# The skip term of a Mamba-2 mixer: from TensorE's products with a diagonal to a ScalarE copy and GpSimd arithmetic

## The chip, the cores and the metric

The kernel runs on one NeuronCore of a Trainium2 chip, as one program. The metric is the device time in microseconds (us), the median of three runs. The core has five instruction streams: TensorE (PE, matrix products into PSUM), VectorE (DVE), ScalarE (ACT), GpSimd (POOL) and SyncE (SP, which issues most DMAs). Each executes its own instructions in the order in which they are written; between engines, an instruction waits on semaphores that others raise.

## The reference, cut to what matters

One transformer block on `x` of shape (2, 4096, 256): an adaptive layer norm, a Mamba-2 mixer with a gated linear unit (GLU) and a layer norm, a gated residual, then a mixture-of-experts layer with 16 experts, 4 chosen per token. The change touches only the mixer's skip term. There `xs` (512 channels, 8 heads of 64) comes out of a causal convolution and a SiLU, and a state-space scan runs over each head:

```
h = h * dA[:, :, None, None] + dti[:, :, None, None] * xi[..., None] * Bi[:, None, None, :]
y = jnp.einsum('bhpn,bn->bhp', h, Ci)
...
y = jnp.transpose(ys, (1, 0, 2, 3)) + D_skip[None, None, :, None] * xh      # the skip term
y = y * jax.nn.silu(z)
y = y * jax.lax.rsqrt(jnp.mean(y * y, axis=-1, keepdims=True) + EPS) * rms_w
return y @ W_out
```

`D_skip` is one number per head, so the skip term scales each head's 64 channels of `x` by one number.

## The kernel before, in words

The program has four stages. The first prepares weights and the normed, transposed input (0 to about 150 us). The second is the mixer, to about 1250 us; the change lies there. The third runs the experts on rows gathered by DMA, and the fourth adds everything up.

The mixer works on groups of 256 tokens, 16 groups for each of the two sequences (b = 0, 1), each group cut into two chunks of 128 tokens (c = 0, 1). Its order of work is written out by hand. The function `halves` calls `half(first, second, tail, ...)` once for each step of a pipeline, and every engine has its own `half`, which says in which order that engine does its parts. In one half three groups are in flight: `first` is projected and convolved, `second` runs the scan, and `tail` does the output projection, the GLU and the second norm. The sequences take turns, so there are 32 halves with a `second`. Other arguments add routing work: `routed` groups get their expert logits, `chosen` picks the experts for two groups at once (every other half, from group 3 on), and `sent` scatters a group's rows to the experts' tables with eight indirect DMAs that GpSimd issues (`scatter`, from group 4 on).

I call the 13 halves with both `sent` and `chosen` first-kind halves, the 13 with `sent` and no `chosen` second-kind ones, and the six halves of groups 1 to 3 early ones.

Within the scan, chunk-wise: TensorE turns `cv` (x after the convolution, channels on partitions) into x by token in PSUM, in the bank `Q(b, c)`. VectorE makes `xdt` (x times dt) and `xend` from that bank. ScalarE puts exponentials into `dec`, VectorE multiplies them by C·B (`times_decay`), and TensorE's `within` writes the part of y inside the chunk back into `Q(b, c)`. The part of y that comes from the state (`from_state`, bank `Q(b, 2)`) is scaled by VectorE into `yy` (`scale_from_state`). `add_within` adds the bank to `yy`. Then GpSimd multiplies by silu(z) (`gate_y`), ScalarE squares and sums, VectorE scales the sum (`mean_square`), GpSimd takes the root (`root_y`), ScalarE scales y (`norm_y`), and TensorE turns it (`transpose_y`).

Before the change, `within` starts with four fp32 products per chunk: `cv` times `skip_w`, a diagonal of D made in the first stage. They add D·x into the same bank as the rest, so y needs no other instruction for it.

VectorE's order in a half, around the change: `times_decay` 0, `scale_from_state` 0, `new_state` 0 (waits for GpSimd's `decay_state`), `times_decay` 1, `add_within` 0, `scale_from_state` 1, `apply2` of the tail (two instructions from PSUM, L1452, then two from SBUF, L1459), `mean_square` 0, `add_within` 1, `conv` of the first group's pair 0, `mean_square` 1. TensorE's `project_xbc` 1 waits for `apply2`.

## Time and profile before

| | us |
|---|---|
| median of 3 runs | 1898.64 (1896.55 to 1900.88) |
| the profiled execution | 1901.73 |
| its span, first to last instruction | 1899.9 |
| TensorE busy, whole span | 1612.4 (85%) |
| VectorE busy | 1337.1 (70%) |
| ScalarE busy | 1113.9 (59%) |
| GpSimd busy | 990.0 (52%) |

A profile records one execution. An instruction's row has a start and a duration; a row of several instructions that follow each other on an engine shows their count and their joint duration. The duration of an instruction that waited inside the engine for a resource contains this wait. Idle time before an instruction is given in brackets with what ended it. In the page's second part the span is cut into 40 slices of 47.5 us, each digit a tenth.

### The profile page before, as it was taken

The numbers are of one execution on the slowest core, as the hardware profiler recorded it, in microseconds if no ns is written. First come the engines' busy times: TensorE is split into PE (matmuls) and PEld (weight loads), VectorE is DVE, ScalarE is ACT, GpSimd is POOL, SyncE is SP. The second block draws the span as 40 slices with busy tenths as digits, with TensorE's granted clock in tenths as the row PEclk, the third lists the DMA queues.
The fourth block names the chain that finished last, engine by engine and source line by source line (L and its number), as shares of the span: only waits on it lengthen the run. The fifth ranks groups of instructions, "written<-read, shape, count | busy, mean of one in ns | idle before, by whom it ended". The sixth has DMA issues, their size and how long they took to land. (4 is left out here: it accounts for less than half of the span.)

```text
span 1899.9 us, 36188 instructions
## 1 busy us (share of the span) xinstructions
PE 1612.4 (85%) x10868; PEld 1389.8 (73%) x10868; DVE 1337.1 (70%) x3293; ACT 1113.9 (59%) x2270; POOL 990.0 (52%) x938
## 2 busy tenths in 40 slices
PE   6752899999999999999999999742999999995877
PEld 5751677777787777777777777631999999993554
DVE  6641688888888888888888888534555555553777
ACT  2322576767767676767767676533777777771211
POOL 1200333465656566565656565655666666673332
PEclk8556999999999999999999999855999999996999
DMA  7413010121212212121212121157766666647785
GB/s 255 155 47 118 15 43 32 48 72 61 78 61 74 68 60 76 66 71 64 77 59 78 64 64 67 62 189 207 231 202 213 213 200 212 212 137 300 293 303 210
DMA packets 147626, 240.27 MB, mean 126 GB/s; under 512 B 25500, under 2 KB 94364, under 8 KB 147136
## 3 DMA queue, kind: packets, MB, share of 16 engines
q1 hardware_dynamic: 122096, 168.45, 27.5%
q0 software_dynamic: 25344, 69.50, 10.1%
q8 instruction: 97, 1.59, 0.4%
q14 instruction: 89, 0.73, 0.1%
HBM read 130.51 MB, written 109.48 MB: 126 GB/s over the span
## 5 line engine op out<-in xcount | busy, mean ns | idle before, releaser
L2004 POOL DMA_INDIRECT ys_dram<-byo,bids x272 | 260.6, 958 | 141.2 <-ACT byo L1933 98.2
L1358 DVE SCALAR_TENSOR_TENSOR cv<-xc,convw,cv 128x256 f32<-128x256 f32 x576 | 300.4, 589 | 41.3 <-ACT cv L1218 41.3
L912 POOL DMA_INDIRECT xs_dram<-rows,dest x256 | 264.5, 1033 | 77.7 <-issue 66.9
L1966 DVE TENSOR_TENSOR bff<-bgs,bank 128x256 f32<-128x256 f32 x136 | 57.3, 421 | 148.2 <-ACT bgs L1916 148.2
L133 PE MATMUL bank<-wh,bhh 128*128 x544 | 154.3, 284 | 0.0
L135 PE MATMUL bank<-wh,bhl 128*128 x544 | 153.9, 283 | 0.0
L134 PE MATMUL bank<-wl,bhh 128*128 x544 | 153.7, 283 | 0.0
L133 PE MATMUL bank<-hTh,win_hi 128*128 128x256 f32 x384 | 116.2, 303 | 42.6 <-POOL hTl L1543 39.2
L1257 ACT ACTIVATE xdt<-yy 128x512 f32<-128x512 f32 x64 | 40.3, 629 | 158.7 <-POOL yy L1556 158.7
L1556 POOL TENSOR_TENSOR yy<-yy,zs 128x512 f32<-128x512 f32 x64 | 87.7, 1371 | 70.7 <-DVE yy L1399 70.2
L1933 ACT ACTIVATE byo<-bank,bws 128x256 f32<-128x256 f32 x272 | 114.3, 472 | 17.2 <-PE bank L135 1.4
L1086 PE MATMUL bank<-xdt,dec 128*128 128x64 f32 x1024 | 121.6, 272 | 1.7 <-DVE dec L1384 1.7
L1957 DVE TENSOR_TENSOR bhl<-bank,bhh 128x512 fp32r<-128x512 f32 x136 | 94.1, 692 | 38.5 <-ACT bhh L1909 23.6
L1086 PEld LDWEIGHTS bank<-xdt,dec 128*128 128x128 f32 x1024 | 119.5, 192 | 2.1 <-DVE dec L1384 2.1
L133 PEld LDWEIGHTS bank<-hTh,win_hi 128*128 128x128 f32 x384 | 73.3, 191 | 57.7 <-issue 50.9
L1842 PE MATMUL bank<-ident,bx 128*128 128x128 f32 x544 | 82.6, 275 | 32.2 <-DMA bx<-xs_dram 32.2
L134 PE MATMUL bank<-hTl,win_hi 128*128 128x256 f32 x384 | 109.1, 284 | 0.0
L135 PE MATMUL bank<-hTh,win_lo 128*128 128x256 f32 x384 | 109.0, 284 | 0.0
L1218 ACT ACTIVATE cv<-bank,convb,convw 128x256 f32<-128x256 f32 x192 | 97.7, 562 | 10.5 <-PE bank L135 10.5
L133 PEld LDWEIGHTS bank<-wh,bhh 128*128 128x128 f32 x544 | 103.1, 189 | 0.4 <-issue 0.4
L134 PEld LDWEIGHTS bank<-wl,bhh 128*128 128x128 f32 x544 | 103.1, 190 | 0.0
L135 PEld LDWEIGHTS bank<-wh,bhl 128*128 128x128 f32 x544 | 103.0, 189 | 0.0
(262 smaller groups left out, 5343.8 us busy)
## 6 DMA issues: line engine op xcount, KB each, us to landing
bx<-xs_dram SPq DMA_DIRECT2D x272, 129.0 KB
cy<-ys_dram SPq DMA_DIRECT2D x32, 1024.0 KB, 8.3
px<-in_x SPq DMA_DIRECT2D x16, 512.0 KB
h_t<-phT SPq DMA_DIRECT2D x16, 512.0 KB, 4.0
hT<-h_t SPq DMA_DIRECT2D x32, 256.0 KB
xr<-in_x SPq DMA_DIRECT2D x32, 256.0 KB
x_dram<-xr SPq DMA_DIRECT2D x32, 256.0 KB, 2.0
h_dram<-h SPq DMA_DIRECT2D x32, 256.0 KB, 2.5
```

The lines of the kernel that those rows point to most:

```text
L133: pe.matmul(out, a_hi, b_hi, start=start, stop=False, skip_group_check=True)
L134: pe.matmul(out, a_hi, b_lo, start=False, stop=False, skip_group_check=True)
L135: return pe.matmul(out, a_lo, b_hi, start=False, stop=stop, skip_group_check=True)
L912: pool.indirect_dma_start(out=xs_dram[:, :], out_offset=bass.IndirectOffsetOnAxis(ap=dest[p][:, CH * b + c, k:k + 1], axis=0), in_=rows[b] ...
L1086: last = pe.matmul(Q(b, c)[:, h * HD:(h + 1) * HD], dec[b][:, c, h, :], xdt[b][:, c, h * HD:(h + 1) * HD], start=False, stop=True, skip_gr ...
L1218: last = act.activation(cv[b][:, n, :], Q(b, pair)[:, m * GROUP:(m + 1) * GROUP], ACT.Identity, bias=convb[:, n:n + 1], scale=convw[:, n, ...
L1358: dve.scalar_tensor_tensor(cv[b][:, m, :], xc[b][:, m, tap:tap + GROUP], convw[:, m, tap:tap + 1], cv[b][:, m, :], ALU.mult, ALU.add).then ...
L1556: pool.tensor_tensor(y, y, zs[b][:, c, :], ALU.mult).then_inc(y4_done[b], 1)
L1842: last = pe.transpose(XT[u % 2][:, (k * 2 + n) * P:(k * 2 + n + 1) * P], x[u % XBUF][:, n, k * P:(k + 1) * P], ident[:, :])
L1933: last = act.activation(yo[u % YBUF][:, n, :], DN[u % 2][:, n * D:(n + 1) * D], ACT.Copy, scale=ws[u % XBUF][:, n:n + 1])
L1957: dve.tensor_tensor(hl[u % 2][:, :, :, :].rearrange("p k n t -> p (k n t)"), XT[u % 2][:, :], hh[u % 2][:, :, :, :].rearrange("p k n t -> ...
L2004: pool.indirect_dma_start(out=ys_dram[:, :], out_offset=bass.IndirectOffsetOnAxis(ap=ids[u % XBUF][:, n:n + 1], axis=0), in_=yo[u % YBUF][ ...
```

## The change

ScalarE copies x by token from `Q(b, c)` to a new SBUF tile `skip` (4 KiB a partition, shared by both sequences). GpSimd multiplies it in place by D per head (`times_skip`) and adds it to the state's part of y in `yy` (`add_skip`). TensorE's `within` no longer has the four products; its first product opens the bank. VectorE's `add_within` waits for `add_skip` instead of for its own `scale_from_state`. GpSimd's scatter of six rows is cut into four before the scan's parts and two after them. In the first stage four VectorE instructions that made the diagonal are gone, and a constant of 8 columns is loaded in place of one of 4.

```diff
 def prepare_tokens
-                        for m in range(KI):
-                            dve.tensor_scalar(skip_w[:, m, :], ident[:, :], dcol[:, m:m + 1], None, ALU.mult)
...
 within (PE)
                     pe.wait_ge(xend_done[b], CH * i + c + 1)
-                    for m in range(KI):
-                        pe.matmul(Q(b, c)[:, m * P:(m + 1) * P], cv[b][:, m, c * P:(c + 1) * P], skip_w[:, m, :],
-                                  start=(m == 0), stop=False, skip_group_check=True)
+                    pe.wait_ge(xk_done[b], CH * i + c + 1)
                     pe.wait_ge(w_done[b], CH * i + c + 1)
                     for h in range(H):
                         last = pe.matmul(Q(b, c)[:, h * HD:(h + 1) * HD], dec[b][:, c, h, :],
-                                         xdt[b][:, c, h * HD:(h + 1) * HD], start=False, stop=True,
+                                         xdt[b][:, c, h * HD:(h + 1) * HD], start=(h == 0), stop=True,
...
 ACT
+                def copy_x(b, i, c):
+                    act.wait_ge(xend_done[b], CH * i + c + 1)
+                    act.wait_ge(skip_done[1 - b], 2 * CH * (i + b))
+                    act.activation(skip[:, c, :], Q(b, c)[:, :], ACT.Copy).then_inc(xk_done[b], 1)
...
                     if second:
                         decays(*second, 1)
-                    if second:
+                        copy_x(*second, 0)
+                        copy_x(*second, 1)
                         copy_b(*second)
...
 add_within (DVE)
-                    dve.wait_ge(y1s_done[b], CH * i + c + 1)
+                    dve.wait_ge(skip_done[b], 2 * CH * i + CH + c + 1)
                     dve.wait_ge(yin_ps[b], CH * i + c + 1)
...
 POOL
+                def times_skip(b, i, c):
+                    pool.wait_ge(xk_done[b], CH * i + c + 1)
+                    x = skip[:, c, :].rearrange("p (h e) -> p h e", h=H)
+                    pool.tensor_tensor(x, x, d_head[:, :].unsqueeze(2).to_broadcast([P, H, HD]),
+                                       ALU.mult).then_inc(skip_done[b], 1)
+
+                def add_skip(b, i, c):
+                    pool.wait_ge(skip_done[b], 2 * CH * i + c + 1)
+                    pool.wait_ge(y1s_done[b], CH * i + c + 1)
+                    pool.tensor_tensor(yy[b][:, c, :], yy[b][:, c, :], skip[:, c, :], ALU.add).then_inc(skip_done[b], 1)
...
                     if sent:
-                        scatter(pool, *sent, slice(2, 8))
+                        scatter(pool, *sent, slice(2, 6))
                     if early:
                         scatter(pool, *early, slice(0, EARLY))
                     if second:
+                        times_skip(*second, 0)
+                        times_skip(*second, 1)
                         decay_state(*second, 0)
                     if tail:
                         root_norm2(*tail)
                     if second:
+                        add_skip(*second, 0)
                         gate_y(*second, 0)
+                        add_skip(*second, 1)
                         root_y(*second, 0)
                         gate_y(*second, 1)
                         root_y(*second, 1)
+                    if sent:
+                        scatter(pool, *sent, slice(6, 8))
```

GpSimd's order in one half with `sent`, from the second scatter call, which follows `shift_x`, to the next `decay_state`, before. `state` is `decay_state`, `rs` the roots of the norms, `yy<-yy,zs` is `gate_y`, `rr` is `root_y`, DMA is a scatter:

```order
L912 DMA xs_dram<-rows,dest 135168x258 x6
L1550 TENSOR_TENSOR state<-state,par 128x512
L900 TENSOR_TENSOR rs<-rs,minus_half 128x2
L1556 TENSOR_TENSOR yy<-yy,zs 128x512
L900 TENSOR_TENSOR rr<-rr,minus_half 128x1
L1556 TENSOR_TENSOR yy<-yy,zs 128x512
L900 TENSOR_TENSOR rr<-rr,minus_half 128x1
L1550 TENSOR_TENSOR state<-state,par 128x512
```

The same stretch in the changed kernel. `skip<-skip,d_head` is `times_skip`, `yy<-yy,skip` is `add_skip`:

```order
L912 DMA xs_dram<-rows,dest 135168x258 x4
L1560 TENSOR_TENSOR skip<-skip,d_head 128x512 x2
L1554 TENSOR_TENSOR state<-state,par 128x512
L900 TENSOR_TENSOR rs<-rs,minus_half 128x2
L1566 TENSOR_TENSOR yy<-yy,skip 128x512
L1571 TENSOR_TENSOR yy<-yy,zs 128x512
L1566 TENSOR_TENSOR yy<-yy,skip 128x512
L900 TENSOR_TENSOR rr<-rr,minus_half 128x1
L1571 TENSOR_TENSOR yy<-yy,zs 128x512
L900 TENSOR_TENSOR rr<-rr,minus_half 128x1
L912 DMA xs_dram<-rows,dest 135168x258 x2
L1554 TENSOR_TENSOR state<-state,par 128x512
```

Two scatters have moved from before the scan's parts to behind `root_y` 1, ahead of the tail's `decay_state`. Two products stand before `decay_state` 0, one sum between the root and `gate_y` 0, and one sum between `gate_y` 0 and `root_y` 0.

TensorE's order from the tail's `transpose_y2` (`y`) through `from_state` (`state,cv`), `state_add` (`xend,bg`) and `within` (`xdt,dec`) to the first product of `project_xbc` 1 (L133), before:

```order
L1143 MATMUL bank<-ident,y 128x128 x4
L1097 MATMUL bank<-state,cv 128x512
L1104 MATMUL bank<-xend,bg 128x512
L1082 MATMUL bank<-skip_w,cv 128x128 x4
L1086 MATMUL bank<-xdt,dec 128x64 x8
L1097 MATMUL bank<-state,cv 128x512
L1082 MATMUL bank<-skip_w,cv 128x128 x4
L1086 MATMUL bank<-xdt,dec 128x64 x8
L133 MATMUL bank<-hTh,win_hi 128x256
```

And in the changed kernel:

```order
L1141 MATMUL bank<-ident,y 128x128 x4
L1095 MATMUL bank<-state,cv 128x512
L1102 MATMUL bank<-xend,bg 128x512
L1084 MATMUL bank<-xdt,dec 128x64 x8
L1095 MATMUL bank<-state,cv 128x512
L1084 MATMUL bank<-xdt,dec 128x64 x8
L133 MATMUL bank<-hTh,win_hi 128x256
```

The four products per chunk are gone; nothing else has moved on TensorE. On ScalarE the two copies stand between the exponentials of chunk 1 and `copy_b`, and VectorE's order in the mixer is the same as before.

## Rows read from the trace of the kernel before

**Rows 1.** The page's busy shares and the granted clock in 40 slices.
```profile
PE 1612.4 (85%) x10868; PEld 1389.8 (73%) x10868; DVE 1337.1 (70%) x3293; ACT 1113.9 (59%) x2270; POOL 990.0 (52%) x938
...
PEclk8556999999999999999999999855999999996999
```

**Rows 2.** Busy us of each engine in 650 to 850 us (columns: us; engines; clock).
```profile
650.00:850.00 200.00, 186.51 (x1255) 154.40 (x1256) 171.71 (x417) 141.16 (x282) 121.56 (x117) 1.00 0.21 69
```

**Rows 3.** Groups by line, 400 to 1100 us: count, busy us, mean ns, idle.
```profile
L1082 PE MATMUL bank<-skip_w,cv 128*128 128x128 f32 x336 | 44.3, 275 | 0.0
```

**Rows 4.** ScalarE in order of time: start, duration, instruction, idle before it.
```profile
715.09 0.60 ACT L1242 ACTIVATE bg<-bank 128x512 f32<-128x512 f32 x1 [1.04 <-PE bank L1049]
```

**Rows 5.** VectorE in order of time, a first-kind half, then a second-kind one.
```profile
720.67 0.69 DVE L1405 TENSOR_TENSOR state<-state,bank 128x512 f32<-128x512 f32 x1 [0.40 <-POOL state L1550]
721.27 1.22 DVE L1384 TENSOR_TENSOR dec<-dec,bg 128x1024 f32<-128x1024 f32 x1
722.41 0.68 DVE L1399 TENSOR_TENSOR yy<-yy,bank 128x512 f32<-128x512 f32 x1
...
724.51 0.88 DVE L1459 SCALAR_TENSOR_TENSOR xr<-sg,rs,xr 128x256 f32<-128x256 f32 x2
...
725.56 0.69 DVE L1399 TENSOR_TENSOR yy<-yy,bank 128x512 f32<-128x512 f32 x1
726.16 3.51 DVE L1358 SCALAR_TENSOR_TENSOR cv<-xc,convw,cv 128x256 f32<-128x256 f32 x6
...
753.64 0.69 DVE L1405 TENSOR_TENSOR state<-state,bank 128x512 f32<-128x512 f32 x1 [1.41 <-POOL state L1550]
...
755.38 0.68 DVE L1399 TENSOR_TENSOR yy<-yy,bank 128x512 f32<-128x512 f32 x1
...
758.34 0.68 DVE L1399 TENSOR_TENSOR yy<-yy,bank 128x512 f32<-128x512 f32 x1
```

**Rows 6.** GpSimd in order of time, the same two halves.
```profile
719.07 1.49 POOL L1550 TENSOR_TENSOR state<-state,par 128x512 f32<-128x512 f32 x1
720.53 0.72 POOL L900 TENSOR_TENSOR rs<-rs,minus_half 128x2 f32<-128x2 f32 x1
723.17 1.27 POOL L1556 TENSOR_TENSOR yy<-yy,zs 128x512 f32<-128x512 f32 x1 [1.92 <-DVE yy L1399]
...
726.32 1.48 POOL L1556 TENSOR_TENSOR yy<-yy,zs 128x512 f32<-128x512 f32 x1 [0.24 <-DVE yy L1399]
...
750.06 0.96 POOL L912 DMA_INDIRECT xs_dram<-rows,dest  x1 [0.30 <-issue]
...
752.49 1.05 POOL L1550 TENSOR_TENSOR state<-state,par 128x512 f32<-128x512 f32 x1
```

**Rows 7.** TensorE in order of time, the same two halves.
```profile
723.55 1.90 PE L1086 MATMUL bank<-xdt,dec 128*128 128x64 f32 x16
...
758.41 0.39 PE L133 MATMUL bank<-hTh,win_hi 128*128 128x256 f32 x1 [0.28 <-DVE xr L1459]
```

**Rows 8.** VectorE: a conv pass alone, a `dec` product that waited, all of L1358 (min/median/max).
```profile
700.93 2.47 DVE L1358 SCALAR_TENSOR_TENSOR cv<-xc,convw,cv 128x256 f32<-128x256 f32 x6
...
652.08 2.60 DVE L1384 TENSOR_TENSOR dec<-dec,bg 128x1024 f32<-128x1024 f32 x1
...
L1358 DVE SCALAR_TENSOR_TENSOR cv<-xc,convw,cv x576: 468/477/1722, 182.7 to 1198.3; 128x256 f32<-128x256 f32 x192
```

**Rows 9.** GpSimd's state decay behind VectorE's `dec` product, an early half.
```profile
293.81 1.91 POOL L1550 TENSOR_TENSOR state<-state,par 128x512 f32<-128x512 f32 x1 [5.63 <-PE bank L1097]
```

**Rows 10.** VectorE in the same early half.
```profile
293.60 1.22 DVE L1384 TENSOR_TENSOR dec<-dec,bg 128x1024 f32<-128x1024 f32 x1
...
295.83 0.69 DVE L1405 TENSOR_TENSOR state<-state,bank 128x512 f32<-128x512 f32 x1 [0.40 <-POOL state L1550]
...
297.57 0.68 DVE L1399 TENSOR_TENSOR yy<-yy,bank 128x512 f32<-128x512 f32 x1
...
300.86 0.69 DVE L1399 TENSOR_TENSOR yy<-yy,bank 128x512 f32<-128x512 f32 x1 [0.24 <-PE bank L1086]
```

14 lines of the change are left out of this document (8 added, 6 removed).

## The prediction, made before the changed kernel ran

> **What bounds the kernel now.** I began with the busy shares and the clock. TensorE is the busiest engine, 85% of the span, and in the mixer every slice but the first ones shows its full granted clock [rows 1]. A stretch in the middle of the mixer gives 186.5 us of TensorE in 200, VectorE 171.7, ScalarE 141.2, GpSimd 121.6 [rows 2]. So TensorE looks like the bound, and GpSimd looks 39% free. Both shares mislead, and the next views show why.
>
> The timeline tells which wait ends last. TensorE starts `project_xbc` 1 at 758.41 when VectorE's `apply2` releases it [rows 7]. In the first-kind half it ends `within` 1 at 725.45 (723.55 + 1.90) [rows 7], as `apply2` ends at 725.39 (724.51 + 0.88) [rows 5]. VectorE meanwhile goes from instruction to instruction with little idle time, and waits 0.40 and 1.41 us before `new_state` 0 for GpSimd's `decay_state` [rows 5]. So the path through this part of a half is VectorE's queue with GpSimd's in it: `decay_state` 0, `new_state` 0, `times_decay` 1, `add_within` 0, `gate_y` 0, the squares, `mean_square` 0, `add_within` 1, then the convolution and everything of the next half behind it. I measure by three marks, each a VectorE start: s = `new_state` 0, a = `add_within` 0, e = `add_within` 1. In the first-kind half a - s is 1.74 and e - a is 3.15; in the second-kind half 1.74 and 2.96 [rows 5]; in the early half 1.74 and 3.29 [rows 10].
>
> There is a second thing that no busy share shows. A VectorE instruction with both inputs in SBUF and a GpSimd tensor instruction do not run together. A convolution pass of six instructions takes 2.47 us alone [rows 8], and 3.51 us [rows 5] where `gate_y` 1 (726.32, 1.48 us) lies beside it [rows 6]. The difference is 1.04 us, and the median of these instructions is 0.477 us with a longest one of 1.722 [rows 8]. It goes the other way too: `decay_state` takes 1.05 us where VectorE waits idle [rows 5, 6], but 1.91 us behind `times_decay` 0, which starts 0.21 us before it and lasts 1.22 [rows 9, 10]; it ends 0.90 us after it. Where VectorE reads PSUM nothing waits: `gate_y` 0 takes 1.27 us [rows 6]. Durations of busy engines contain such waits, so the 39% are not free.
>
> **What is removed.** Eight products a half leave TensorE. The group has 336 records in 21 halves and 44.3 us of busy time [rows 3], 2.11 us a half, 67.5 us over 32 halves. Inside the half they lie ahead of the two `within`, and TensorE then waits for `times_decay` or for `apply2`. Neither s nor a depends on them. Mark e does in some halves: if the product before `within` 1 goes, this release comes about 0.9 us earlier, but I find below that GpSimd then releases later. So I count 0 for the removal. The four VectorE instructions of the first stage and the constant's size are nothing that a row could show.
>
> **ScalarE's two copies.** They cost like `copy_b`, 0.60 us each with some overlap, 1.1 us together, and stand where ScalarE waits 1.04 us for TensorE before `copy_b` at 715.09 [rows 4]. They push `copy_b` by about 0.1 us. Its reader `times_decay` 0 comes over 2 us later. I count 0. Without that gap it would be 1.1 us of ScalarE, which has idle time later in the half.
>
> **GpSimd, up to s.** The two `times_skip` are products of the form of `decay_state` (128x512, one factor broadcast): 1.05 alone, up to 1.49 where it meets VectorE [rows 6]. They take the time of two scatters, 2.43 us (750.06 to 752.49) [rows 6], so GpSimd's queue itself is even. But scatters ran beside VectorE without delaying it, and the products don't. In the second-kind half `times_skip` 0 would run from about 749.8 to 750.8, when VectorE reaches `times_decay` 0 (about 750.4). Two orders are possible. If VectorE gets its turn after the first product, `decay_state` ends about 0.23 us later than now. If GpSimd keeps on through the second product and `decay_state`, VectorE's product and the scaling behind it come first before s, 0.8 us late. A row shows the second kind of order: at 652.08 `times_decay` took 2.60 us, 1.38 too many, behind GpSimd [rows 8]. In the first-kind half the products end at about 718.6, as `times_decay` 0 begins, and the same two orders give 0.08 and 0.55. I take 0.3 and 0.4 for the two kinds, the nearer to the smaller, since the waiting case occurs once in this trace. In early halves GpSimd is idle before `decay_state`, 5.63 us [rows 9], and I take 0.
>
> The Trainium skill ("SBUF — State Buffer", section "Who interferes with whom") says that the pair of SBUF ports shared by VectorE and GpSimd goes to whichever instruction issues first, for its whole length. The row at 652.08 is no clean case of that. By the page alone this term would be 0.08 and 0.23, and the sum 5 us smaller.
>
> **From s to a.** Now `root_norm2` (0.72 us, 720.53) ends at 721.25 [rows 6], where VectorE starts `times_decay` 1 (721.27) [rows 5], and `add_within` 0 follows at 722.41. After the change `add_skip` 0 issues at that same moment, and `add_within` 0 needs both. Both read two SBUF tiles, so they run one after the other. `add_skip` has the form of `gate_y`: 1.27 us [rows 6]. With GpSimd first, VectorE's product is delayed by that less its own start, 1.05. With VectorE first, `add_skip` ends 1.12 us after it (the 0.90 measured above plus the 0.22 by which it is longer), and with 0.1 us for the semaphore and the 0.08 by which VectorE's own instructions overlap, `add_within` 0 is 1.31 us late. I take 1.2, between ends that are close, for all 32 halves.
>
> **From a to e.** `gate_y` 0 starts 0.76 us after a (723.17 - 722.41) and ends at a + 2.03 [rows 5, 6]. `add_skip` 1 follows at once, and `apply2`'s two SBUF instructions start at a + 2.10 (724.51) [rows 5]. They wait until `add_skip` 1 ends at a + 3.3, which costs what the convolution loses to `gate_y` now, 1.04. Where nothing else delayed e it stood at a + 2.96, so e becomes a + 4.0: later by 1.04 in second-kind halves, 0.85 in first-kind and 0.71 in early ones. If VectorE went first, `add_skip` 1 would end after `apply2`, at about a + 4.2, and add 0.2. TensorE's release of `project_xbc` 1 moves with `apply2`, so none of this is taken up there.
>
> **Behind e.** `root_y` 0 now stands behind `add_skip` 1, but ends in time for `gate_y` 1, which waits for e anyway. The two moved scatters (2.4 us) come behind `root_y` 1, and then the tail's `decay_state`. In the second-kind half this ends near VectorE's next SBUF convolution, and could cost up to 0.5 there. VectorE has idle time behind this convolution, so I take 0 and keep 0.5 for the upper end.
>
> **The sum.** Early halves: 1.2 + 0.71 = 1.9 us. First-kind: 0.3 + 1.2 + 0.85 = 2.35. Second-kind: 0.4 + 1.2 + 1.04 = 2.65. Then 6 x 1.9 + 13 x 2.35 + 13 x 2.65 = 11.4 + 30.6 + 34.5 = 76.4 us. Against the profiled execution, 1901.73 (span 1899.9), that is 1978. The median of the runs is 3.1 us below this execution; carried over, the forecast is 1975 us. With all lower ends the halves are 1.76, 1.98 and 2.32, together 66.5 us. With all upper ends they are 1.31 + 0.91 = 2.22, 0.55 + 1.31 + 1.05 = 2.91 and 0.8 + 1.31 + 1.24 + 0.5 = 3.85, together 101 us. The likeliest case's own range is 1965 to 2000.
>
> **The rivals.**
> *No exclusion for the new instructions.* If the sums ran beside VectorE, the chain on GpSimd would still be longer. a would move to the end of `add_skip` 0, s - 0.1 + 0.72 + 1.27 + 0.1 = s + 2.0, 0.25 late, and e to a + 3.4, 0.1 to 0.45 late. With 0.5 us a half over 32 halves that is 16 us: 1915. Against it stand the convolution and `decay_state` rows; for it only that no row shows `add` against `times_decay`. 8%.
> *The collisions partly hide.* One of the two sums finds a gap, because the halves settle into other phases. Then a half loses 1.0 to 1.3 us, 37 us, 1936. 10%.
> *TensorE is the bound.* The share of 93% [rows 2] speaks for it, and the wait of `add_within` 1 for `within` in early halves, where e - a is 3.29 [rows 10]. If all 2.11 us came off each half, 1831 us. It decides if GpSimd's four new instructions end before VectorE needs them, that is if `add_skip` 0 ends by s + 1.7; it issues at s + 0.6 and lasts 1.27. TensorE's waits for `apply2` speak against it. 4%.
> *The clock falls.* TensorE has longer pauses afterwards: one of about 2 us between `within` 1 and `project_xbc` 1, another before `within` 1. Its granted clock is at 2.4 GHz through the mixer now, at half of that in the slices around 1235 to 1330, behind the mixer's end where TensorE is little used [rows 1]. If one half in four ran at 1.2 GHz, its 28.6 us of TensorE (186.5 / 200 of the 32.97 between the two a of rows 5, less 2.11) would take 57, some 22 us over its new length of 35.4, and 8 such halves would bring 176 us on top of the forecast: 2151. No row in the steady part shows a fall. 3%.
> The Trainium skill ("TensorE: Matmul & The Clock Gate", Part 1) says that activity releases the throttle and idleness brings it back; pauses within a busy half are neither clearly, and the page alone doesn't move my chance.
>
> **How the numbers follow.** The forecast has 75%, the rivals 25% together. From 1936 to 2000 lie the forecast's own range and half of the partly hidden case; the 3 us on top are the distance between the profiled execution and the median. The range is 1936 to 2003. What a measurement of this kernel can tell from no change is about 0.2%, 3.8 us. Faster: the TensorE case, 4%. Within: 1%, an exclusion-free case in which the removal helps. Slower: 95%.
>
> **What would show it.** In the changed profile: L1560 and L1566 on GpSimd, 64 each, of 1.05 to 1.5 and 1.27 to 2.4 us. `times_decay` or `add_skip` 0 longer by about 1 us in every half. The second pair of `apply2` near 1.9 us in place of 0.88. a - s near 2.9 and e - a near 4.0. The distance from one a to the next up from 32.97 (755.38 - 722.41) by about 2.5 us. TensorE's busy time down by some 65 us and its share with it, waiting for `times_decay` and `apply2`. The third and fourth stage unchanged. It is wrong if e - a stays near 3.2, if `add_within` 1 waits for TensorE, or if the granted clock falls inside the mixer.

## The result: slower by 6.3%, more than forecast

The changed kernel took 2022.25 us (2014.30 to 2026.90, four runs) against 1899.76 (1896.55 to 1902.91, four runs) of the kernel before beside it: a ratio of 1.063, 95% interval 1.061 to 1.066. That is +122.5 us. I had forecast +76, with a range that ended at 2003. The direction was right, the size was not.

The page of the changed kernel: busy shares, and the granted clock in 40 slices (here of 50.6 us).

```profile
PE 1654.0 (82%) x10356; PEld 1407.0 (70%) x10356; DVE 1426.5 (70%) x3289; ACT 1144.6 (57%) x2334; POOL 1160.0 (57%) x1066
...
PEclk8556998998989898899889997865699999997999
```

The clock row is the surprise. Before, the mixer's slices showed 9 throughout [rows 1]; now many show 8. The windows of the changed kernel (span of the stretch, busy us of PE, PEld, DVE, ACT, POOL, then the clock):

```profile
650.00:850.00 200.00, 177.39 (x1053) 145.15 (x1052) 170.39 (x382) 135.47 (x271) 139.74 (x127) 0.90 0.20 63
216.00:700.00 484.00, 421.85 (x2544) 342.58 (x2545) 404.77 (x880) 317.35 (x628) 298.00 (x268) 0.92 0.16 50
700.00:1200.00 500.00, 437.82 (x2612) 355.81 (x2611) 427.04 (x933) 329.92 (x657) 350.12 (x317) 0.91 0.19 61
```

Before, all of these stretches had 1.00 ([rows 2] for the first). The trace shows the clock at 2.4 GHz (1.0) or at 1.2 GHz (0.5) and nothing between, so a mean of 0.92 over 484 us is 2 x 0.08 x 484 = 77 us at the lower level, and 0.91 over 500 is 90: 167 us in 29 stretches, 3 to 10 us long. I call this sum, always from 216 to 1200 us of a trace, "half clock" below. Before it was 0.

Nearly all of the loss lies in the mixer. The last mark e stood at 1216.4 before and stands at 1335.8 now, 119.4 us of the 124.0 by which the span grew. The two halves' VectorE rows, here a second-kind half, answer to [rows 5]:

```profile
737.94 0.25 DVE L1446 BATCH_NORM_AGGREGATE mv<-st 128x2 f32<-128x6 f32 x2
738.23 2.54 DVE L1449 TENSOR_SCALAR rs<-mv 128x2 f32<-128x2 f32 x1
740.67 1.21 DVE L1388 TENSOR_TENSOR dec<-dec,bg 128x1024 f32<-128x1024 f32 x1
...
742.41 0.67 DVE L1409 TENSOR_TENSOR state<-state,bank 128x512 f32<-128x512 f32 x1
743.00 1.98 DVE L1388 TENSOR_TENSOR dec<-dec,bg 128x1024 f32<-128x1024 f32 x1
745.78 0.69 DVE L1403 TENSOR_TENSOR yy<-yy,bank 128x512 f32<-128x512 f32 x1 [0.81 <-PE bank L1084]
747.53 0.69 DVE L1395 TENSOR_TENSOR yy<-bank,par 128x512 f32<-128x512 f32 x1 [1.06 <-PE bank L1095]
...
749.04 1.27 DVE L1463 SCALAR_TENSOR_TENSOR xr<-sg,rs,xr 128x256 f32<-128x256 f32 x2
...
750.29 0.67 DVE L1403 TENSOR_TENSOR yy<-yy,bank 128x512 f32<-128x512 f32 x1
```

GpSimd in the same half, against [rows 6]:

```profile
737.69 2.04 POOL L1560 TENSOR_TENSOR skip<-skip,d_head 128x512 f32<-128x512 f32 x2
739.69 1.03 POOL L1554 TENSOR_TENSOR state<-state,par 128x512 f32<-128x512 f32 x1
740.84 1.63 POOL L900 TENSOR_TENSOR rs<-rs,minus_half 128x2 f32<-128x2 f32 x1
742.63 1.26 POOL L1566 TENSOR_TENSOR yy<-yy,skip 128x512 f32<-128x512 f32 x1 [0.16 <-DVE yy L1395]
746.55 1.26 POOL L1571 TENSOR_TENSOR yy<-yy,zs 128x512 f32<-128x512 f32 x1 [2.65 <-DVE yy L1403]
748.36 1.27 POOL L1566 TENSOR_TENSOR yy<-yy,skip 128x512 f32<-128x512 f32 x1 [0.55 <-DVE yy L1395]
```

TensorE, the scan's products only, against [rows 7], and the window around them:

```profile
742.03 3.64 PE L1084 MATMUL bank<-xdt,dec 128*128 128x64 f32 x16 [2.88 <-DVE dec L1388]
745.47 2.02 PE L1095 MATMUL bank<-state,cv 128*128 128x512 f32 x2
747.28 2.42 PE L1084 MATMUL bank<-xdt,dec 128*128 128x64 f32 x16
```

```profile
738.00:748.00 10.00, 7.12 (x25) 5.15 (x24) 8.10 (x9) 2.68 (x8) 6.88 (x6) 0.68 0.04 13
```

Read the three engines together. A tiny instruction of VectorE, the `rs` that ends the tail's `norm2` (128x2, ahead of `times_decay` 0), takes 2.54 us: it ends with GpSimd's two `times_skip` and `decay_state`, which follow each other without a gap from 737.69 to 740.72. `times_decay` 0 starts 2.4 us late behind it. TensorE, which no longer has its four products to do ahead of `within` 0, stands still for 2.88 us until `dec` is there. Then its clock falls: the 16 records of `within` 0 (two for each product) take 3.64 us where they took 1.90 [rows 7], `from_state` 1 takes 2.02 (1.08 in a row of another run below), and now VectorE waits for TensorE, 0.81 and 1.06 us, at two places where, the first half aside, it had waited 0.2 us at most. The collision of the sum with `times_decay` 1 (743.00, 1.98 us) is there as well.

Over all halves, the means of the distances between the marks, in us (the tail's `new_state` to s, s to a, a to e, e to the next tail's `new_state`):

| halves | before | changed | difference |
|---|---|---|---|
| 6 early | 11.44, 1.84, 3.33, 14.98 | 11.76, 2.61, 3.90, 16.31 | 0.32, 0.77, 0.57, 1.33 |
| 13 first-kind | 12.83, 1.74, 3.17, 15.55 | 13.47, 2.53, 4.34, 16.50 | 0.64, 0.79, 1.17, 0.95 |
| 13 second-kind | 12.51, 1.76, 3.01, 15.26 | 13.28, 3.01, 4.73, 15.74 | 0.77, 1.25, 1.72, 0.48 |

Times the counts: 20 us up to s (forecast 9), 31 from s to a (forecast 38), 41 from a to e (forecast 29), 27 behind e (forecast 0). The sum is 119. The groups between 400 and 1100 us, the changed kernel (count | busy us, mean ns | idle before):

```profile
L1388 DVE TENSOR_TENSOR dec<-dec,bg 128x1024 f32<-128x1024 f32 x38 | 69.8, 1838 | 0.0
L1566 POOL TENSOR_TENSOR yy<-yy,skip 128x512 f32<-128x512 f32 x38 | 48.2, 1267 | 10.1 <-DVE yy L1395 10.0
L1560 POOL TENSOR_TENSOR skip<-skip,d_head 128x512 f32<-128x512 f32 x38 | 38.9, 1051 | 0.4
L1449 DVE TENSOR_SCALAR rs<-mv 128x2 f32<-128x2 f32 x19 | 25.5, 1344 | 0.7
L1463 DVE SCALAR_TENSOR_TENSOR xr<-sg,rs,xr 128x256 f32<-128x256 f32 x38 | 25.4, 708 | 0.7
```

and the same three VectorE groups before:

```profile
L1384 DVE TENSOR_TENSOR dec<-dec,bg 128x1024 f32<-128x1024 f32 x42 | 52.7, 1255 | 0.1
...
L1459 DVE SCALAR_TENSOR_TENSOR xr<-sg,rs,xr 128x256 f32<-128x256 f32 x42 | 18.5, 482 | 0.7
...
L1445 DVE TENSOR_SCALAR rs<-mv 128x2 f32<-128x2 f32 x21 | 3.6, 169 | 0.9 <-DVE mv L1442 0.2
```

The instruction on which I had spent no word, `rs`, lost 1.18 us a piece, as much as both `times_decay` of a half together (2 x 0.58). The mean hides two cases: in steady second-kind halves `rs` takes 2.53 us and `times_decay` 0 its usual 1.21, in first-kind ones `rs` takes 0.28 and `times_decay` 0 takes 2.13. GpSimd's new instructions took 1.05 and 1.27 us, as forecast: where they collide, it is VectorE that waits. GpSimd waits too, but elsewhere: the root at 740.84, beside `times_decay` 0, took 1.63 us (0.72 in [rows 6]).

### The profile page after: what moved, and what is told of

It reads as the page before. It is cut to its first block and busy times, and to the rows that moved or that the text cites. A ratio compares the mean times of both kernels' runs of the same rounds, so it can differ in the third digit from the quotient of the medians.

```text
span 2023.9 us, 35548 instructions
## 1 busy us (share of the span) xinstructions
PE 1654.0 (82%) x10356; PEld 1407.0 (70%) x10356; DVE 1426.5 (70%) x3289; ACT 1144.6 (57%) x2334; POOL 1160.0 (57%) x1066
## 5 line engine op out<-in xcount | busy, mean ns | idle before, releaser
L912 POOL DMA_INDIRECT xs_dram<-rows,dest x256 | 271.2, 1059 | 74.5 <-issue 64.9
L1084 PEld LDWEIGHTS bank<-xdt,dec 128*128 128x128 f32 x1024 | 166.0, 249 | 117.9 <-issue 117.9
L1084 PE MATMUL bank<-xdt,dec 128*128 128x64 f32 x1024 | 166.7, 333 | 61.7 <-DVE dec L1388 61.7
L133 PE MATMUL bank<-hTh,win_hi 128*128 128x256 f32 x384 | 129.8, 338 | 63.3 <-POOL hTl L1547 39.8
L133 PE MATMUL bank<-wh,bhh 128*128 x544 | 154.3, 284 | 0.2 <-issue 0.2
L133 PEld LDWEIGHTS bank<-hTh,win_hi 128*128 128x128 f32 x384 | 88.1, 230 | 78.0 <-issue 51.6
L1954 ACT ACTIVATE byo<-bank,bws 128x256 f32<-128x256 f32 x272 | 114.3, 472 | 17.2 <-PE bank L135 1.4
L135 PE MATMUL bank<-hTh,win_lo 128*128 128x256 f32 x384 | 121.5, 316 | 0.0
L134 PE MATMUL bank<-hTl,win_hi 128*128 128x256 f32 x384 | 121.4, 316 | 0.0
L1388 DVE TENSOR_TENSOR dec<-dec,bg 128x1024 f32<-128x1024 f32 x64 | 114.2, 1784 | 7.1 <-ACT bg L1240 7.1
L133 PEld LDWEIGHTS bank<-wh,bhh 128*128 128x128 f32 x544 | 103.1, 189 | 0.6 <-issue 0.6
```

What stands on the lines that cost most here:

```text
L133: pe.matmul(out, a_hi, b_hi, start=start, stop=False, skip_group_check=True)
L134: pe.matmul(out, a_hi, b_lo, start=False, stop=False, skip_group_check=True)
L135: return pe.matmul(out, a_lo, b_hi, start=False, stop=stop, skip_group_check=True)
L912: pool.indirect_dma_start(out=xs_dram[:, :], out_offset=bass.IndirectOffsetOnAxis(ap=dest[p][:, CH * b + c, k:k + 1], axis=0), in_=rows[b] ...
L1084: last = pe.matmul(Q(b, c)[:, h * HD:(h + 1) * HD], dec[b][:, c, h, :], xdt[b][:, c, h * HD:(h + 1) * HD], start=(h == 0), stop=True, skip ...
L1388: dve.tensor_tensor(dec[b][:, c, :, :], dec[b][:, c, :, :], bg[b][:, 1, c, :].unsqueeze(1).to_broadcast([P, H, P]), ALU.mult).then_inc(w_d ...
```

## The experiments

They ran on five chips, and the number of the first pair's chip is not on record; by its times I take it for a sixth and call it the first chip. On the five the kernel before took 2070.4, 2069.9, 2102.4, 2099.3 and 2067.3 us, so kernels are compared by their ratio to the kernel before on their own chip, and by marks and half clock from their profile. A difference between ratios from two chips is less certain than one on the same chip. "Moved" stands for the kernel before with two of six scatters behind `root_y` 1, and nothing else.

**Both kernels again.** No edit.

> The kernel before, unchanged, profiled on the chip of these runs: on the chip of the last runs it took 2070 us in place of 1900, and I want its mixer there. Port and clock theory alike: the mixer's last add_within 1 starts near 1216 us after the start if the chip differs only behind the mixer; if this chip lets the clock fall in the mixer of the kernel before too, then later, near 1280, with stretches of 0.5 in the granted clock between 216 and 1200 us.

> The changed kernel, unchanged, on the same chip. Its distance to the kernel before is 122 us on the first chip. If the clock falls in both kernels on this chip, the distance shrinks to that of the port collisions and the longer chain, 50 to 90 us; if in the changed one alone, it stays 110 to 130.

Measured: the kernel before 2069.27 (ratio 0.9998, 0.997 to 1.003), the changed one 2129.38, ratio 1.028 (1.020 to 1.036), or +59.5 us. The distances of the changed kernel are within 0.8 us of the first chip's (half clock 137 us, last e 1331.9). It is the kernel before that differs there: 15.16 us from tail to s in first-kind halves in place of 12.83, 48 us of half clock, the last e at 1277 in place of 1216. So the change costs half as much on these chips, since something that it contains helps there. The next experiment says what.

**Two scatters moved, nothing else.**

```diff
-                        scatter(pool, *sent, slice(2, 8))
+                        scatter(pool, *sent, slice(2, 6))
...
                         root_y(*second, 1)
+                    if sent:
+                        scatter(pool, *sent, slice(6, 8))
```

> The kernel before with nothing but the move of two scatters from ahead of decay_state 0 to behind root_y 1. GpSimd then reaches decay_state 0 about 2.4 us earlier, and VectorE's wait of 1.41 us for it in second-kind halves shrinks to the 0.4 of the others: 13 halves by 1.0 us, 13 us less, 1884 to 1890, faster than both kernels. If the moved scatters delay the next half (the tail's decay_state lands on VectorE's convolution, up to 0.5 us a second-kind half), 1890 to 1896. The rival that moved scatters are part of the change's loss expects more than 1905.

> The kernel before with the two scatters moved, again, as the baseline of this group: its mixer had no clock fall and the marks of the first chip's kernel before (last add_within 1 at 1218.8 against 1216.4). Expected there again within 4 us, whichever chip it is.

Measured: 2013.60, ratio 0.972 (0.969 to 0.975), and on another chip 2044.14, ratio 0.973 (0.970 to 0.977). Tail to s is 12.9 and 13.2 us in first-kind halves, half clock 0 and 3, the last e at 1218.8 and 1233.5: the mixer is nearly back at the length that the kernel before has on the first chip. (The second time I had expected the last e within 4 us of 1218.8; it came 15 later.) This is the version that beats both kernels here, by 57 us the kernel before and by 116 the changed one (2129.38 - 2013.60, from two chips whose kernels before were within 1 us). Whether it helps on the first chip was not run; the mixer of the kernel before is as short there without it (1216.4), which speaks against it. Of the 34 us by which VectorE's idle time between 400 and 1100 us differs, the largest part, 17.5, lies ahead of the tail's `norm2`, whose first group is this, the kernel before on these chips and then moved (the second run):

```profile
L1437 DVE BATCH_NORM_STATS2 st<-bank 128x6 f32<-128x256 f32 x40 | 15.3, 423 | 52.5 <-remote 45.3 <-issue 3.8 <-PE bank L1143 3.3
```

```profile
L1437 DVE BATCH_NORM_STATS2 st<-bank 128x6 f32<-128x256 f32 x42 | 16.0, 423 | 35.0 <-remote 24.2 <-PE bank L1143 10.7
```

On the first chip this group waits 15.7 us, all for L1143. What "remote" hides, and why chips differ, I could not settle.

**The removal alone.**

```diff
-                    for m in range(KI):
-                        pe.matmul(Q(b, c)[:, m * P:(m + 1) * P], cv[b][:, m, c * P:(c + 1) * P], skip_w[:, m, :], ...)
...
-                                         xdt[b][...], start=False, stop=True,
+                                         xdt[b][...], start=(h == 0), stop=True,
```

> The kernel before without TensorE's products with the diagonal and with nothing in their place, so the skip term is left out of y. It does one part of the change alone. My prediction said that the products are off the path: within 0.2% of before, 1896 to 1904 us, and TensorE's granted clock stays full through the mixer. The clock theory (the products covered TensorE's wait for times_decay 0, and without them the pause lets the clock fall) in its strong form expects falls here too, some 27 us of 1.0 and then 3.4 to 10 us of 0.5 in each half, and 10 to 40 us more than before. In its weak form the pause needs the late times_decay as well: then this kernel is like before. TensorE as the bound would give 1830 to 1870.

> The kernel with the two scatters moved, without TensorE's products with the diagonal and nothing in their place (the skip term is left out): the removal alone on the undisturbed baseline. Clock theory in its strong form (the products' cover alone holds the clock): stretches at half clock in most halves, 60 to 125 us of them between 216 and 1200, and the last add_within 1 20 to 60 us later than in the baseline. Prediction's view (off the path): within 5 us of it and no fall. Early halves of the run without products on the six-scatter kernel showed a to e 0.34 shorter, so a small gain, 5 to 10 us, is possible where the clock holds.

Measured: on the unmoved kernel 2093.89, ratio 1.012 (1.008 to 1.015), with 130 us of half clock; on the moved one 2057.12, ratio 0.979 (0.976 to 0.983), 13 us over moved alone on the same chip, half clock 58 in place of 3. Taking 67 us of TensorE's work away makes the kernel slower. `within` of the moved kernel, then without the skip products:

```profile
L1086 PE MATMUL bank<-xdt,dec 128*128 128x64 f32 x662 | 80.1, 274 | 8.8 <-DVE dec L1384 8.8
```

```profile
L1083 PE MATMUL bank<-xdt,dec 128*128 128x64 f32 x640 | 89.3, 300 | 20.5 <-DVE dec L1381 20.5
```

The work that is gone has become a wait for `dec` (20.5 us in place of 8.8), and the products behind it are slower by the clock. The only gain is where I had looked for it: in early halves a to e is 2.99 in place of 3.33.

**The clock given back.** The changed kernel with products with zeros in place of the four that left, then with 12 and 8 of them in place of 4 and 4.

```diff
+                    for n in range((4, 4)[c]):
+                        m = n % KI
+                        pe.matmul(Q(b, c)[:, m * P:(m + 1) * P], cv[b][:, m, c * P:(c + 1) * P], zeros[:, :],
+                                  start=(n == 0), stop=False, skip_group_check=True)
```

> The changed kernel with TensorE's eight products a half put back, with a zero matrix in place of the diagonal, so TensorE has the instructions of before and y is that of the changed kernel. Clock theory: TensorE works through a part of its wait for times_decay 0 (2.9 us idle in the changed kernel, then about 2), the clock falls less often, and the time comes down from 2022 towards the forecast of port collisions alone, 1975 to 2000. Port-only theory (all of the excess is VectorE waiting for GpSimd): no change or slower, 2022 to 2035, since products only add work.

> The changed kernel with 12 zero products ahead of within 0 and 8 ahead of within 1, 20 a half instead of the 8 of before, so that TensorE is busy through the whole wait for times_decay 0. Clock theory: the granted clock is full through the mixer as in before (mean above 0.92), and the time is that of the port collisions alone, 1970 to 1990, though TensorE does more work than ever. Port-only theory: slower than the changed kernel, over 2022.

Measured: 2115.70, ratio 1.022 (1.019 to 1.026), and 2102.27, ratio 1.016 (1.013 to 1.020), against 1.028 of the changed kernel. Half clock is 82 and then 0 us, from 137 in the changed kernel; the last e stands at 1320.0 and 1305.1, from 1331.9. The windows of the kernel with more products:

```profile
216.00:700.00 484.00, 453.56 (x3154) 382.13 (x3153) 417.01 (x902) 325.92 (x644) 309.27 (x277) 1.00 0.16 52
700.00:1200.00 500.00, 470.19 (x3289) 397.84 (x3288) 441.49 (x969) 340.69 (x679) 360.15 (x326) 1.00 0.20 64
```

Useless products make the kernel faster by 24 us (by the ratios, of two chips; on one chip, 12 and 8 products against 4 and 4, by 13 us), because they keep TensorE from standing still ahead of `within`. e to the next tail falls from 16.3 and 17.3 to 14.9 and 15.3 in early and first-kind halves. Part of that is only moved, since the filling makes a to e 4.43 us in both kinds, but halves of one trace say the same: behind e, first-kind halves of the changed kernel take 15.7 us where no half clock falls there, and 16.8 to 17.2 where some 3 us of it do. The 27 us that the mixer gained are a lower bound of the clock's part, since the filling delays something too, as the next run shows. And most of the cost is not the clock: with none of it at half, this kernel is 89 us over moved alone on the same chip (2102.27 - 2013.60).

**Without the sums.** The moved scatters, copies and `times_skip`, `gate_y` and `add_within` as before, zeros on TensorE; then with more zeros.

```diff
                 def add_within(b, i, c):
-                    dve.wait_ge(skip_done[b], 2 * CH * i + CH + c + 1)
+                    dve.wait_ge(y1s_done[b], CH * i + c + 1)
...
-                        add_skip(*second, 0)
                         gate_y(*second, 0)
-                        add_skip(*second, 1)
```

> The changed kernel with the four zero products per chunk on TensorE and without GpSimd's two sums, so the skip term is left out; the copies, GpSimd's two products and the moved scatters stay. My prediction's terms expect only term C, up to s: 0.3 and 0.4 us a half, some 9 us over before. From the changed trace (tail's new_state to s 0.64 and 0.77 later) the port theory expects 10 to 30 us over before, with s to a 1.74 and a to e 2.96 to 3.3 as before. If the products starve VectorE's small rs instruction in each half (2.5 us in place of 0.17), that shows here undiminished.

> The changed kernel without the two sums (skip term left out) and with 12 and 8 zero products on TensorE ahead of the two within, so that the clock should hold: the price of GpSimd's two products and the longer start alone. Its twin with 4 and 4 zero products ended its mixer 53 us after the baseline, with 51 us of half clock. Port theory: tail's new_state to s 0.5 to 0.9 longer, the rest as in the baseline, 15 to 25 us later than it. If more TensorE work alone delays a or e, 25 to 50.

Measured: 2063.38, ratio 0.996 (0.992 to 0.999), and 2120.93, ratio 1.009 (1.006 to 1.012). The first is 0.024 or 50 us above moved alone, of which I had forecast 9, with 55 us of half clock. The second was meant to show the rest at full clock and failed at that: VectorE's `add_within` waits 44.7 us for `within` (5.5 in the kernel with the same filling and the sums), so the filling itself had become the bound.

**Products and copies apart.** The first of those two kernels without its copies (the first two lines of the diff; `times_skip` then waits for `xend`), then without its products (the last two).

```diff
-                        copy_x(*second, 0)
-                        copy_x(*second, 1)
...
-                        times_skip(*second, 0)
-                        times_skip(*second, 1)
```

> The moved scatters and the two times_skip of GpSimd, each waiting for xend and not for a copy; no copies on ScalarE, no sums; TensorE's eight products a half stay, with zeros. The skip term is left out. It splits the term that I forecast at 0, 0.3 and 0.4 us a half (9 us in all) and that came to about 50 us between the moved scatters alone (ratio 0.972) and copies with products (0.996). Theory: GpSimd's products, back to back with decay_state, keep VectorE's small rs instruction and times_decay 0 waiting, and TensorE's pause behind them costs clock: then nearly all of it is here, ratio 0.990 to 0.997, tail to s 0.3 to 0.8 us longer than with moved scatters alone, a to e of second-kind halves near 5, 30 to 60 us of half clock. Rival: the copies on ScalarE do it, since within waits for them and copy_b comes later: then this kernel is within 0.4% of the moved scatters alone, 0.970 to 0.977.

> The moved scatters and ScalarE's two copies, for which within waits; no products and no sums on GpSimd; TensorE's eight products a half stay, with zeros. The skip term is left out. Theory (the cost is on GpSimd): within 0.4% of the moved scatters alone, ratio 0.970 to 0.977, no half clock, all three marks as there within 0.1 us. Rival (the cost is on ScalarE): ratio 0.985 to 0.996, copy_b and with it times_decay 0 late by the copies' 1.1 us, tail to s longer by 0.5 to 1.

Measured: products alone 2068.47, ratio 1.000 (0.997 to 1.003), half clock 55, last e 1272.7; copies alone 2015.51, ratio 0.975 (0.970 to 0.980), half clock 7, last e 1225.8. The copies cost nothing that can be told from moved alone. The products cost 53 us over the copies on the same chip: by the marks 23 us up to s, 5 from s to a and 21 from a to e. A half with products alone, VectorE and TensorE:

```profile
742.04 0.28 DVE L1448 TENSOR_SCALAR rs<-mv 128x2 f32<-128x2 f32 x1
742.23 2.14 DVE L1387 TENSOR_TENSOR dec<-dec,bg 128x1024 f32<-128x1024 f32 x1
```

```profile
744.42 2.00 PE L1090 MATMUL bank<-xdt,dec 128*128 128x64 f32 x16 [0.56 <-DVE dec L1387]
746.26 1.08 PE L1101 MATMUL bank<-state,cv 128*128 128x512 f32 x2
```

This is a first-kind half, where GpSimd's three instructions (740.24 to 743.28) meet `times_decay` 0 only, and it loses 0.9 us. In second-kind halves they meet `rs`, and the groups say what that costs, products alone and then copies alone:

```profile
L1448 DVE TENSOR_SCALAR rs<-mv 128x2 f32<-128x2 f32 x20 | 23.9, 1197 | 0.7
```

```profile
L1454 DVE TENSOR_SCALAR rs<-mv 128x2 f32<-128x2 f32 x21 | 5.4, 255 | 0.7
```

This trace also prices the clock, since its second-kind halves differ in little else. Their lengths, from one tail's `new_state` to the next, up to 1200 us:

| half clock in the half | halves | length, us |
|---|---|---|
| none | 3 | 33.5 to 33.9 |
| some 3 us | 4 | 35.1 to 35.3 |
| some 7 us | 4 | 36.8 |

So 3 us at half clock cost 1.65 us here and 7 us cost 3.3, in these eight halves 20 us of the 53.

**Products and scatters interleaved.** The zeros kernel with a scatter behind each product, so that no two of them follow back to back.

```diff
-                        scatter(pool, *sent, slice(2, 6))
+                        scatter(pool, *sent, slice(2, 5))
...
                         times_skip(*second, 0)
+                    if sent:
+                        scatter(pool, *sent, slice(5, 6))
...
                         times_skip(*second, 1)
+                    if sent:
+                        scatter(pool, *sent, slice(6, 7))
...
                         decay_state(*second, 0)
...
-                        scatter(pool, *sent, slice(6, 8))
+                        scatter(pool, *sent, slice(7, 8))
```

> The changed kernel with four zero products per chunk on TensorE, and with GpSimd's two products pulled apart by scatters (product, scatter, product, scatter, decay_state; one scatter left behind root_y 1), so that they no longer stand back to back ahead of decay_state. Port-and-starvation theory: VectorE's rs and times_decay 0 get their turn between, tail's new_state to s is unchanged or longer by one scatter (13.3 to 14.5), but times_decay 0 is on time, TensorE's pause before within 0 falls below 1 us, and the clock holds in more halves: 15 to 45 us less than the same kernel without the interleaving (2115.7 where before was 2070). If the port cost is the same in every order: within 10 us of it.

Measured: 2157.20, ratio 1.028 (1.024 to 1.033), no gain over the zeros kernel's 1.022. A miss, and the trace says where it went. VectorE's and GpSimd's rows in a second-kind half:

```profile
745.60 1.30 DVE L1455 TENSOR_SCALAR rs<-mv 128x2 f32<-128x2 f32 x1
746.82 1.21 DVE L1394 TENSOR_TENSOR dec<-dec,bg 128x1024 f32<-128x1024 f32 x1
...
750.10 0.69 DVE L1415 TENSOR_TENSOR state<-state,bank 128x512 f32<-128x512 f32 x1 [1.47 <-POOL state L1560]
```

```profile
745.81 1.05 POOL L1566 TENSOR_TENSOR skip<-skip,d_head 128x512 f32<-128x512 f32 x1
747.03 1.88 POOL L914 DMA_INDIRECT xs_dram<-rows,dest  x1 [0.17 <-issue]
748.94 1.06 POOL L1560 TENSOR_TENSOR state<-state,par 128x512 f32<-128x512 f32 x1
```

`rs` now waits for one product, not for three instructions: 1.30 us, the longest of 32 is 1.55 in place of 2.54, and their mean between 400 and 1100 us is 714 ns. So the row without a gap was indeed what made the wait long. But the scatter put behind the second product delays `decay_state`, for which `new_state` then waits 1.47 us, and with one scatter more ahead of the scan tail to s is 15.85 us in first-kind halves (13.40 in the zeros kernel). The run changed two things at once, and the gain of one was lost to the other. I had also expected the clock to hold in more halves. TensorE's pause ahead of `within` 0 did shrink, from 1.34 us to 0.30 in second-kind halves and from 0.39 to nothing in first-kind ones, yet half clock stayed, 89 us (82 in the zeros kernel). Its 26 stretches now begin in other pauses or within 1 us behind them: 11 in first-kind halves in a wait of 4 us for VectorE's `y` ahead of `transpose_y2`, behind the additional scatter, and 15 in a wait of 1.4 to 1.9 us ahead of `project_xbc` 1 for `apply2`, which the sums delay.

**The sums alone**, of a tile of zeros, with TensorE's products in place: on the unmoved kernel, on the moved one, and there sum 0 and sum 1 each by itself.

```diff
                 def add_within(b, i, c):
-                    dve.wait_ge(y1s_done[b], CH * i + c + 1)
+                    dve.wait_ge(skip_done[b], CH * i + c + 1)
...
+                def add_skip(b, i, c):
+                    pool.wait_ge(y1s_done[b], CH * i + c + 1)
+                    pool.tensor_tensor(yy[b][:, c, :], yy[b][:, c, :], skip[:, :], ALU.add).then_inc(skip_done[b], 1)
...
+                        add_skip(*second, 0)
                         gate_y(*second, 0)
+                        add_skip(*second, 1)
```

> The kernel before with GpSimd's two sums added, of a tile of zeros, so y is right, and add_within waiting for them; no copies, no products on GpSimd, no scatter moved, TensorE's products kept. Port theory: s to a grows by 0.75 to 1.3 and a to e by 0.7 to 1.0 in each half, together 50 to 65 us over before. A chain without exclusion: 10 to 25 us.

> The kernel with the two scatters moved plus GpSimd's two sums of a tile of zeros, TensorE's products kept. My terms A and B: s to a 1.05 to 1.31 longer, a to e 0.7 to 1.0 longer in each half, 60 to 75 us over the baseline if all of it reaches the end, with e to the tail's next new_state unchanged. Clock theory adds that the later times_decay lets the clock fall in some halves (e to next grows above 15.5, half-clock stretches of over 40 us in total). Without exclusion: 10 to 25 us.

> The two scatters moved plus the sum of chunk 0 alone (zeros). Term A alone: s to a 1.05 to 1.31 longer in my forecast, 0.75 to 0.9 by the run with both sums; 25 to 35 us over the kernel with moved scatters.

> The two scatters moved plus the sum of chunk 1 alone (zeros). Term B alone: a to e 0.5 to 1.04 longer, 15 to 30 us over the kernel with moved scatters.

Measured: 2135.39, ratio 1.029 (1.020 to 1.038); 2099.97, ratio 0.999 (0.997 to 1.001); 2056.38, ratio 0.980 (0.976 to 0.985); 2060.30, ratio 0.983 (0.978 to 0.987). Over moved alone (0.973) that is 56 us for both sums, on the same chip, and some 14 and 20 for one, by ratios of two chips. By the marks, sum 0 makes s to a 0.8 longer and leaves a to e at 3.0; sum 1 makes a to e 3.92 and leaves s to a at 1.8. These are the two mechanisms of the forecast, each alone at its place. The groups of both sums on the moved kernel, then of moved alone:

```profile
L1387 DVE TENSOR_TENSOR dec<-dec,bg 128x1024 f32<-128x1024 f32 x40 | 65.0, 1624 | 0.0
...
L1462 DVE SCALAR_TENSOR_TENSOR xr<-sg,rs,xr 128x256 f32<-128x256 f32 x40 | 36.7, 957 | 0.7
```

```profile
L1384 DVE TENSOR_TENSOR dec<-dec,bg 128x1024 f32<-128x1024 f32 x42 | 51.0, 1215 | 0.0
...
L1459 DVE SCALAR_TENSOR_TENSOR xr<-sg,rs,xr 128x256 f32<-128x256 f32 x40 | 17.6, 482 | 0.7
```

`times_decay` waits 0.41 us a piece, 0.82 a half, and `apply2`'s pair takes 1.91 in place of 0.96, the "near 1.9" of the forecast. That both cost more together (56) than apart (34) comes with 38 us of half clock, which each alone has 10 to 14 of. In the trace with both, second-kind halves are 34.1 to 34.2 us long without half clock and mostly 35.4 with 3 us of it; at such a price its 10 stretches are worth some 13 of the 22 us. That is an estimate, and the rest was not tested apart.

## Why the forecast was right in direction and 46 us short

**What failed.** Two steps of the prediction failed. The larger is the clock: its fall had 3% and no term in the sum, and the 0 for the removal and the 0 behind e rested on its holding. The smaller is GpSimd up to s, where I took 0.3 and 0.4 us a half and the runs showed 0.55 and 0.87. The 22 halves from the seventh to the 28th, 11 of each kind, tell the two apart, since the changed kernel shows each distance both with half clock in it and without. Without, they are 13.29, 2.50, 3.92 and 15.70 us in first-kind halves and 13.40, 2.49, 3.92 and 14.91 in second-kind ones (where every second-kind half has half clock on the first chip, from s to a and from a to e, the value is that of its trace on the other chip). Sums over the 22 halves, changed less before, in us:

| | forecast | measured | at full clock | the clock's part |
|---|---|---|---|---|
| up to s | 7.7 | 14.4 | 14.4 | 0 |
| s to a | 26.4 | 22.8 | 16.6 | 6.2 |
| a to e | 20.8 | 32.3 | 18.7 | 13.6 |
| behind e | 0 | 11.7 | 1.9 | 9.8 |
| sum | 54.9 | 81.1 | 51.6 | 29.5 |

The last two columns are an estimate by difference. The kernel with 12 and 8 zero products, which has no half clock in these halves, supports it: it is 55.7 us over the first chip's kernel before in them. So at full clock the forecast's sum was met, and that is luck in part: up to s it was half of the measured value, from s to a half as much again. In the other ten halves the changed kernel lost 38 us where the forecast has 21; the second to the sixth each have 3 to 7 us of half clock as well, but I have not divided these.

**The sum of the parts.** On the other chips both sums cost 56 us, the products 53, the removal 13, the copies nothing, and the moved scatters give back 57 to 58. The first three make 122 us, and the change cost 122.5 on the first chip; with the scatters' gain they make 65, and it cost 59.5 there. Parts taken from several kernels need not add, and each of the three has half clock in it, so the agreement is better than it deserves; that the gain is missing on the first chip is argued from the length of the mixer, not run.

**From s to a, and from a to e: the mechanism held, the first size did not.** The sums meet `times_decay` 1 and `apply2` as the steps said. They were forecast at 38 + 29 us and cost 56 where they stand alone on a steady kernel, some of it the clock's. s to a came to some +0.75 at full clock where I had 1.2 (`add_skip` 0 issues 0.4 us ahead of the product, at 742.63 against 743.00 in the rows above, and that much of it lies under other work), and to 1.25 in second-kind halves, with TensorE at half clock. The prediction's lower end of 1.05 does not follow from its rows either: 1.27 less the 0.02 between 721.25 and 721.27 is 1.25. a to e is 3.92 us at full clock, where the forecast had 4.0. In the changed kernel `apply2`'s mean of 0.71 us shows less of the second collision than forecast, since VectorE's other waits spread the two apart; where a to e is longer than 3.92 it is for another reason, TensorE at half clock.

**GpSimd up to s: the second step that failed.** I took 0, 0.3 and 0.4 us a half, 9 us in all, and it was 20 by the marks; the products alone cost 23 up to s and 53 in all, the rest behind s, with TensorE late and at half clock. Of the two orders that I weighed, GpSimd keeping on through `decay_state` gave 0.55 and 0.8, and each of the 22 steady halves shows it (12.74 to 13.29, and 12.53 to 13.40 us, in the usual half of each kind). I took the smaller for likelier because the waiting case, the row at 652.08 [rows 8], stood once in the trace. And both orders had `times_decay` 0 as VectorE's first instruction to meet the products. The first is `rs`, 0.17 us long and so never looked at. It reads one tile in SBUF and not two, so the rule that I had read from the rows would not have named it. Once it had to wait, it waited through the rest of the first `times_skip`, the second and `decay_state`: not for one instruction, but for all that followed without a gap. The interleaved run, with gaps, halved that wait. Not every VectorE instruction in SBUF is so exposed: the two that make `mv`, at 737.94, ran beside the first `times_skip` and took 0.25 us together, as before (0.25 at the same place). What was counted as two scatters' time against two products' time, "even", exchanged work that collides with nothing for work that collides.
The Trainium skill ("SBUF — State Buffer", "Who interferes with whom") gives the pair of ports to whichever instruction issues first, for its whole length. The row at 738.23 agrees that one waits for the other. But an `rs` that came up during the first `times_skip` would by that rule have its turn behind it, after some 0.5 us (an estimate, from the 2.04 us of the two in the rows above); it let two more instructions pass, and took 2.54 us.

**The removal: forecast 0, and it cost 13 us, or 24 on the unmoved kernel.** "TensorE then waits" was right. That the wait has a price was dismissed with the clock rival's 3%.

**The clock: the rival came in part, and it is the larger step that failed.** I had priced it as one half in four wholly at 1.2 GHz, 176 us. It came as 29 short stretches, most halves having one, 167 us in all, of which the filler runs give back 27 in the mixer and 24 in the median, and the estimate above says 29.5 for 22 halves alone. The price depends on where a stretch falls and on what else is waited for there. Around `within`, 3 us of it cost 1.65 us in the run with products alone, but 0 to 0.4 us in first-kind halves of the changed kernel (35.4 to 35.8 us against 35.4), where, as I read it, the sums hold VectorE anyway; 3 us behind e cost 1.5 there (36.9). The clock row before showed no fall [rows 1], but the products ahead of `within` were what covered TensorE there, and they were what the change took away. I had named pauses between `within` 1 and `project_xbc` 1 and ahead of `within` 1. The first of these came, 1.0 to 1.8 us long, and 8 of the 29 stretches begin in it or within 1 us behind it; the other 21 begin in the pause ahead of `within` 0 or less than 2 us behind it, 1.5 us long in first-kind halves and 2.88 in the row above. That one I had not named.
The Trainium skill ("TensorE: Matmul & The Clock Gate", Part 1) says that idleness brings the throttle back; the rows at 742.03 (3.64 us in place of 1.90) and the filler runs (half clock 137 to 0) agree.

**Behind e: forecast 0, measured 27 us.** Not the moved scatters, as my upper end had it, since moved alone leaves e to tail at 15.0, 15.4 and 15.5; with the clock held, it was 14.9, 15.3 and 15.5 in the changed kernel too.

**The other rivals.** Without exclusion, `times_decay` would have stayed near 1.25 us; it went to 1.84. That collisions partly hide, 37 us in all, is out by the 52 us of 22 halves at full clock. That TensorE is the bound is out by the removal alone, ratio 1.012.

## What to carry to other kernels

Work moved to GpSimd can be paid by VectorE. List every VectorE instruction that can start while GpSimd works in SBUF, the tiny ones too, and ask of each what it would cost if it waited for the whole unbroken run of GpSimd instructions and not for one. Before taking products away from TensorE, look what it will do in their place: if it will wait for another engine, the products are free, and may be holding the clock. Halves of one trace that differ only in the granted clock give its price without another run. And test the parts of a change apart, since one that helps (here two scatters moved, 2.8% by itself) can hide in one that hurts.

## What was unexpected of the hardware

A 128x2 instruction of VectorE took up to 2.54 us (0.17 alone) behind three GpSimd instructions. TensorE's granted clock fell to half within a kernel whose TensorE was busy 87 to 88% of the stretch (421.85 / 484 and 437.82 / 500), in 29 stretches of 3 to 10 us; in the window around the row of 742.03 it was 0.68. The same kernel before took 1900 us on one chip and 2067 to 2102 on others, part of it in the mixer (61 us, most of which an order of the scatters removes) and the rest behind it, for every kernel alike: from the last e to the end of the span 684 and 688 us on the first chip, 786 to 805 on the others. The cause of that stays open.
